# First unit's decay rows read straight from the sums and masked by GpSimd; two weight steps moved

## The reference, cut to what matters

```
proj = hidden_states @ in_proj_w.T                  # gate, xBC, dt
xBC  = silu(depthwise_conv(xBC, 4 taps))            # x, B, C
dt   = clip(softplus(dt + dt_bias), 0.001, 100)
cs   = cumsum(dt * A, inside a chunk of 128 tokens)
Lmat = where(tril, exp(cs[l] - cs[s]), 0)
Y    = ((C B^T) * Lmat) @ (x * dt) + contribution of the chunk before + x * D
out  = groupwise_rms_norm(Y * silu(gate)) @ out_proj_w.T
```

## Time and profile before

| | us |
|---|---|
| median of 3 runs | 2258.12 |
| the profiled execution | 2259.13 |
| its span | 2257.3 |
| PE busy | 2115.1 (94%) |
| DVE busy | 1571.0 (70%) |
| ACT busy | 1187.8 (53%) |
| POOL busy | 806.2 (36%) |

### The profile page before, as it was taken

One profiled execution on the slowest core, in us unless ns is written; L12 is line 12 of the kernel. 1 busy time (PEld: TensorE's weight loads), 2 busy tenths in 40 slices (PEclk: granted clock), 3 DMA queues, 4 the chain that ended last, 5 costly groups with the idle time before them and its releaser, 6 DMA issues. The chain is left out here.

```text
span 2257.3 us, 38134 instructions
## 1 busy us (share of the span) xinstructions
PE 2115.1 (94%) x11176; PEld 1596.0 (71%) x11176; DVE 1571.0 (70%) x3186; ACT 1187.8 (53%) x2846; POOL 806.2 (36%) x680
## 2 busy tenths in 40 slices
PE   6899998998888999999999999999999999987998
PEld 4555555545667777877777787777787787766877
DVE  3666665565688599589589778858958958845345
ACT  4554545413575377377467547647737746642330
POOL 4352523211154145235325425424524533431230
PEclk8799998999999999999999999999999999989999
DMA  6000000002989587697867958758769776602101
GB/s 248 11 1 10 7 1 1 1 0 73 244 212 219 110 230 189 114 230 183 158 184 190 183 141 205 176 114 226 190 108 234 184 147 187 152 22 103 46 10 38
DMA packets 242994, 286.94 MB, mean 127 GB/s; under 512 B 9440, under 2 KB 211424, under 8 KB 242144
## 3 DMA queue, kind: packets, MB, share of 16 engines
q1 hardware_dynamic: 242784, 284.43, 52.3%
HBM read 281.78 MB, written 104.60 MB: 171 GB/s over the span
## 5 line engine op out<-in xcount | busy, mean ns | idle before, releaser
L1719 PE MATMUL b_ps<-xh_keep,wh 128*128 128x512 f32 x1152 | 459.1, 399 | 3.5 <-DVE bc L1497 1.6
L1721 PE MATMUL b_ps<-xh_keep,wl 128*128 128x512 f32 x1152 | 449.7, 390 | 0.0
L1720 PE MATMUL b_ps<-xl_keep,wh 128*128 128x512 f32 x1152 | 449.0, 390 | 0.0
L1408 POOL TENSOR_TENSOR wl<-wraw,wh 128x512 fp32r<-128x512 f32 x144 | 186.8, 1297 | 384.3 <-ACT wh L1202 382.6
L1497 DVE SCALAR_TENSOR_TENSOR xs<-b_ps,par,xs 128x510 f32<-128x510 f32 (+2 forms) x384 | 284.5, 741 | 54.0 <-ACT xs L1223 40.6
L1525 DVE TENSOR_TENSOR decayed<-b_ps,b_scores 128x384 f32<-128x384 f32 x512 | 266.6, 548 | 45.3 <-ACT b_ps L1252 31.1
L1251 ACT ACTIVATE b_ps<-rows,ncs 128x256 f32<-128x256 f32 x512 | 238.9, 467 | 97.5 <-DMA rows<-skewed_rows 65.0
L1719 PEld LDWEIGHTS b_ps<-xh_keep,wh 128*128 128x128 f32 x1152 | 217.1, 188 | 50.0 <-issue 3.6
L1721 PEld LDWEIGHTS b_ps<-xh_keep,wl 128*128 128x128 f32 x1152 | 216.5, 188 | 46.9
L1720 PEld LDWEIGHTS b_ps<-xl_keep,wh 128*128 128x128 f32 x1152 | 217.2, 189 | 42.7
L1616 DVE SCALAR_TENSOR_TENSOR yl<-yg,par,yh 128x512 fp32r<-128x512 f32 x128 | 99.6, 778 | 202.2 <-ACT yh L1265 198.4
(11 more groups left out here) (228 smaller groups left out, 3967.4 us busy)
## 6 DMA issues: line engine op xcount, KB each, us to landing
rows<-skewed_rows SPq DMA_DIRECT2D x256, 384.0 KB, 4.2
skewed_rows<-sum_rows SPq DMA_DIRECT2D x63, 1024.0 KB, 12.1
wraw<-win_dram SPq DMA_DIRECT2D x144, 256.0 KB, 9.4
skewed_rows<-sum_rows SPq DMA_DIRECT2D x63, 512.0 KB, 14.1
qkv_or_out_weights<-wout_dram SPq DMA_DIRECT2D x8, 2048.0 KB, 16.4
w<-w_dram SPq DMA_DIRECT2D x2, 3584.0 KB, 23.3
fraw<-wgu_dram SPq DMA_DIRECT2D x11, 512.0 KB, 3.5
draw<-wd_dram SPq DMA_DIRECT2D x1, 2816.0 KB, 11.7
```

Source lines behind the costliest of these rows:

```text
L1408: nc.gpsimd.tensor_tensor(wl[:, n % RING, :], wraw[:, n % RING, :], wh[:, n % RING, :].bitcast(F32), ALU.subtract).then_inc(w_lo.sem, 1)
L1719: nc.tensor.matmul(out, w_h, x_h, start=(k == 0), stop=False)
L1720: nc.tensor.matmul(out, w_h, x_l, start=False, stop=False)
L1721: last = nc.tensor.matmul(out, w_l, x_h, start=False, stop=(k == KT - 1))
```

## The change

It has three parts, and they touch the start of the block, and the start of every group.

The decay rows of the first unit are no longer staged. `load_first` reads them from `sum_rows` straight into `rows`, every partition the same row (8 DMAs, 256 or 128 KB each, one with 1 KB runs and one with 512-byte runs for each sequence). What lies where l < s is then no longer -1e30, so GpSimd adds it: it makes a tile `below` (0 or -1e30) once, and for each sequence adds it to two blocks of 2 x 128 columns. It does so behind the low part of slice 4, with the low part of slice 5 behind the first sequence.

Slice 6 is loaded ahead of the sums. The wait for the padding moves behind the first rows.

In unit 0 of every group, ACT does the first tap ahead of `weights_hi(g, 6)`.

```
-            for n in range(3, 6):
+            for n in range(3, 7):
                 load_in(0, n)
             sp.wait_ge(sums_ready, 2)
             sp.dma_start(ssm["rows"][:, :, 0:SEQ], csT...).then_inc(kept, 16)
+            sp.wait_ge(kept, 16)
+            for b in range(BATCH):
+                load_first(b)
+            load_in(0, 7)
             sp.wait_ge(padded, 32)
-            sp.wait_ge(kept, 16)
-            for b in (BATCH - 1, *range(BATCH - 1)):
-                stage_first(b)
-            load_in(0, 6)
-            load_in(0, 7)
-            for b in range(BATCH):
-                load_rows(0, b)
             stage(1)
...
+            def load_first(b):
+                src = ssm["rows"].tensor
+                for at, shift, cols in ((0, 0, SEQ), (SEQ, P, P)):
+                    sp.dma_start(rows[:, b, :, at:at + cols],
+                                 bass.AP(tensor=src, offset=b * ROW + shift, ap=[[0, P], [BATCH * ROW, 2], [1, cols]]))\
+                        .then_inc(first_rows[b], 16)
...
-                    if more:
+                    if more and j:
                         weights_hi(g, 6 + 2 * j)
                     if h:
                         tap(ph, gn, h[0], ...)
                     if not j:
+                        weights_hi(g, 6)
                         next(e[0])
                         next(e[0])
...
-            for n in range(6):
+            nc.gpsimd.tensor_scalar(below[:], cst("tri"), 1.0, BIG, ALU.subtract, ALU.mult).then_inc(below_done, 1)
+            for n in range(5):
                 weights_lo(0, n)
+            pool.wait_ge(below_done, 1)
+            for b in range(BATCH):
+                pool.wait_ge(first_rows[b], 32)
+                for at in (0, SEQ):
+                    block = rows[:, b, :, at:at + P]
+                    last_ = nc.gpsimd.tensor_tensor(block, block, below[:]..., ALU.add)
+                last_.then_inc(rows_loaded[b], 16)
+                if b == 0:
+                    weights_lo(0, 5)
```

More of the change, by code:

```diff
@@ L1011, in ssm_layer @@
         ssq = sb("ssq", [P, TOK])
+        below = sb("below", [P, P])
         rs = sb("rs", [P, 3, NT])
@@ L1084, in ssm_layer @@
         staged = [sem(f"staged{k}") for k in range(8)]
-        first_staged = [sem(f"first_staged{b}") for b in range(BATCH)]
+        first_rows = [sem(f"first_rows{b}") for b in range(BATCH)]
+        below_done = sem("below_done")
         sums_ready = sem("d_sums")
@@ L1133, in load_rows @@
                     return
-                if n:
-                    g, j = (n - 1) // UNITS, (n - 1) % UNITS
-                    ph = Phase("loop", g, g) if g < LOOPS else Phase("epi", 0, g)
-                    sp.wait_ge(*bk.filled(ph, f"E{j}_{b}_1"))
-                    sp.wait_ge(staged[n % 8], 32 * ((n - 1) // 8 + 1))
-                else:
-                    for k in (b - 1, b):
-                        sp.wait_ge(first_staged[k % BATCH], 32)
+                g, j = (n - 1) // UNITS, (n - 1) % UNITS
+                ph = Phase("loop", g, g) if g < LOOPS else Phase("epi", 0, g)
+                sp.wait_ge(*bk.filled(ph, f"E{j}_{b}_1"))
+                sp.wait_ge(staged[n % 8], 32 * ((n - 1) // 8 + 1))
                 sp.dma_start(rows[:, b], bass.AP(tensor=ssm["skewed"].tensor, offset=n % STAGED * P * WIDE + b * ROW,
@@ L1446, in steps @@
                         out_weights_lo(g, 0)
-            for n in range(6):
+            nc.gpsimd.tensor_scalar(below[:], cst("tri"), 1.0, BIG, ALU.subtract, ALU.mult).then_inc(below_done, 1)
+            for n in range(5):
                 weights_lo(0, n)
+            pool.wait_ge(below_done, 1)
[3 more added lines that the diff above has]
+                    block = rows[:, b, :, at:at + P]
+                    last_ = nc.gpsimd.tensor_tensor(block, block, below[:].unsqueeze(1).to_broadcast([P, 2, P]), ALU.add)
+                last_.then_inc(rows_loaded[b], 16)
+                if b == 0:
+                    weights_lo(0, 5)
             with nc.Fori(0, LOOPS, engines=bass.OrderedEngineSet([pool.engine]), hint_back_edge=True) as i:
```

5 lines of the change are left out of this document (removed).

## The result

| | before | after |
|---|---|---|
| median, measured together | 2257.06 us (5 runs, 2251.16 to 2258.63) | 2240.04 us (5 runs, 2237.76 to 2247.59) |
| the profiled execution | 2259.13 | 2237.76 |
| its span | 2257.3 | 2235.9 |

The ratio is 0.9935, with a 95% interval of 0.9916 to 0.9954. The two medians lie 17.0 us apart; the ratio takes 14.7 of the 2257.06 us (10.4 to 19.0), and 12.0 were forecast.

A forecast was written before the change was run, and what follows sets the result against it. PE bounds the kernel on average, but a chain of DMA round trips bounds group 0; ending it 11.9 us sooner at no cost takes the median from 2258.1 to 2246.1 us, range 2242.5 to 2252.5.

The forecast's parts named there:

- Part 1, the first rows: Start of group 0: with the copies out of the queue, staging 1 lands at 578.3 instead of 590.23, 11.9 us sooner.
- rival of slow first rows: Start of group 0: first rows as slow as the old copies, 131 GB/s; gain 6.9 us, time 2251.2, chance 0.14.
- Part 2, the next round: Group 0, second round: staging 2 is issued by 580.8 instead of 592.67, so it follows 11.9 us sooner.
- the sign of ACT's gate: Sign of a wrong forecast: staging 2 more than 3 us behind unit 1's rows, held by ACT's use of old rows.
- Both limits: Issue of staging 2: ACT done with unit 0's rows allows 580.8, the landing of staging 1 allows 580.7.
- The rival in which the queue gains more: Group 0's queue: staging 2 starts with its issue, up to 4 us more gain, some 2243.5 us; chance 0.12.
- "still some 8 us": Sign of a right forecast: ACT's wait for rows in unit 2 stays, since rounds keep their 17.4 us pace.
- Part 3, PE isn't the limit: Group 0: PE could end at 672.4, the DMA chain at 682.4; PE's own 7.8 or 8.8 us is not the gain.
- Part 4, the masks: POOL in unit 0: 8 additions of 0.65 us, 5.2 in all, hidden; by the interference rule 11.7 instead of 11.9 us.
- Part 5, the exchange in later groups: Unit 0 of seven later groups: tap ahead of split costs 0, with 1.2 us of cover; 4.3 us if cover were gone.
- The slower rival: ACT's exchange costs 0.6 us in each of 7 later groups and group 0 gains nothing; 2262.4 us, chance 0.05.
- The sum: Whole kernel: group 0's shift of 11.9 us is passed on whole, nothing paid; the median becomes 2246.1 us.

The follow-up runs named there:

- e6: Changed kernel with the 8 DRAM to DRAM copies put back in SP's queue between the first rows and staging 1; 2255.13 us, 1.0008.
- e9: Changed kernel with four extra, waited-for GpSimd additions ahead of each sequence's two masks; 2247.37 us, 0.9967.
- e8: Changed kernel with only the direct first rows: slice 6 loaded behind them again, ACT in its old order; 2240.91 us, 0.9939.
- e3: Changed kernel without ACT's exchange: high part of slice 6 ahead of the tap again in every group; 2248.18 us, 0.9940.
- e10: Changed kernel with group 0's 2 MB of output weights loaded in unit 4 instead of unit 1; 2241.79 us, 0.9949.
- e12: Changed kernel with the second unit's rows also read directly and group 0's output weights loaded in unit 4; 2244.28 us, 0.9953.
- e13: Changed kernel with the second unit's rows also direct, their masks behind the low parts of slices 6 and 7; 2237.59 us, 0.9925.
- e15: Changed kernel, unchanged, third trace and third set of times; 2240.45 us, 0.9940.
- e2: Changed kernel, unchanged, second trace and second set of times; 2248.68 us, 0.9947.
- e4: Kernel before with ACT's exchange alone, tap ahead of the high part of slice 6; 2261.17 us, 0.9998.
- e5: Kernel before with ACT's exchange and slice 6 loaded ahead of the sums, first rows still staged; 2256.07 us, 1.0001.
- e7: Changed kernel with stagings 1 and 2 issued at the start and one more staging in flight in group 0; 2241.85 us, 0.9948.

## Where the prediction was right, and the step that failed

**Part 1, the first rows.** Right. Rows of unit 1 went out at 576.60, where 578.3 was the forecast, with sums that landed 1.5 us sooner; from the sums 18.5 us against 18.7, over three traces 19.1. The sum of bytes left one slice out (slice 8, issued at 566.61 behind staging 1): from 558.08 to 576.60 some 3.7 MB moved (199 GB/s for 18.52 us) where 3.4 were counted, and so the landing in time owes a little to luck. The first rows' own rate shows only in 559.00 to 562.00: 140 GB/s at a DMA share of 0.51, as the copies of before began (126 GB/s at 0.57 in 560.60 to 562.60). With slice 7 and staging 1 behind them the windows are at 206 and 212 GB/s, near the 223 taken. The rival of slow first rows falls by the rows of unit 1, which it had after 583.

**Part 2, the next round.** Right, and as tight as it was said to be. Staging 2 stood 2.4 us behind those rows (579.04), 2.5 in the second trace. In the third it stood 3.7 us behind, over the 3 us that were named as the sign of ACT's gate, and the later rounds took it back. Both limits that were said to lie side by side do: e6 moves the first and e9 the second, and either costs. The rival in which the queue gains more is not seen in its place: the rows of unit 2 go out 11.7 us sooner in the mean, as those of unit 1 (11.5). ACT's wait for them, "still some 8 us", was 5.88, 7.90 and 4.61 us (before 8.34, 9.50 and 7.61). ACT's wait for slice 6 is gone, but e8 shows that it would not have mattered: with a wait of 5.30 us left there, the gain is the same.

**Part 3, PE isn't the limit.** Right by e6. Turn 0 moved by 8.0 us in the mean where 7.8 or 8.8 was said (9.0, 9.0 and 6.1, trace by trace), and the end of the group by more, with the chain.

**Part 4, the masks.** Wrong in size, and without effect on the sum. A pair took 1.40 to 1.43 us when alone, 0.70 each; 0.65 was the estimate. POOL of the changed kernel:

```profile
563.00 1.90 POOL L1452 TENSOR_TENSOR rows<-rows,below 128x256 f32<-128x256 f32 x2 [5.42 <-DMA rows<-sum_rows]
564.85 1.73 POOL L1404 TENSOR_TENSOR wl<-wraw,wh 128x512 fp32r<-128x512 f32 x1
```

DVE beside it:

```profile
563.61 0.68 DVE L1513 SCALAR_TENSOR_TENSOR xs<-tx,xs 128x512 f32<-128x512 f32 x1
564.46 0.98 DVE L1513 SCALAR_TENSOR_TENSOR xs<-tx,xs 128x512 f32<-128x512 f32 x1 [0.16 <-ACT tx L1234]
```

The pair that met DVE took 1.90 instead of 1.40, the split 1.73 instead of 1.29, and one silu 0.98 instead of 0.68. That is the meeting that the rule of the Trainium skill (SBUF — State Buffer, "Who interferes with whom") foretold, at 0.3 us for DVE. The DVE silu at 563.61 ran at its 0.68 inside the pair's span: there it was POOL that lost the 0.5 us.

In six of the twelve traces of kernels with direct rows the meeting went worse (e3, e6, e10, e12, e13, and e15, the third trace of the changed kernel): the two silus of x took 2.85 to 2.96 us together, 1.37 in before. POOL of e15, then DVE, then PE, and a window (columns as in the earlier trace rows):

```profile
563.72 1.74 POOL L1404 TENSOR_TENSOR wl<-wraw,wh 128x512 fp32r<-128x512 f32 x1
```

```profile
564.23 1.78 DVE L1513 SCALAR_TENSOR_TENSOR xs<-tx,xs 128x512 f32<-128x512 f32 x1
```

```profile
567.73 0.70 PE L1763 MATMUL b_ps<-bc 128*128 128x256 f32 x2 [2.33 <-DVE b_scores L1556]
```

```profile
568.60:571.60 3.00, 3.00 (x10) 2.43 (x9) 2.26 (x4) 0.00 (x0) 2.20 (x4) 0.53 1.15 235
```

The silu ends 0.5 us behind the split, so it took 1.1 us more than its 0.68. PE waits 2.31 to 2.44 us in these six traces instead of 1.0, and behind that wait its granted clock is at half, 0.52 to 0.54 over 3 us; with the wait of 1.31 us in e2 it stays at 1.00. The first turn comes 15.9 to 16.0 us after the sums instead of 13.1 to 13.4. So the masks cost PE up to 2.7 us in unit 0, where the prediction's rule came to 0.2. The chain covers it: e15 has its group 1 after 204.1 us and its gain like the others. In these traces staging 2 also stands further behind the rows of unit 1: 3.7 us in e15, 3.4 in e3 and 4.0 in e10, but 2.5 in e6, whose rows come late.

**Part 5, the exchange in later groups.** Right by the times: cost 0, within the interval of e4. The lines of group 1, beside the earlier trace rows:

```profile
758.39 0.78 ACT L1218 ACTIVATE xs<-b_ps,par 128x512 f32<-128x512 f32 x1 [8.99 <-PE b_ps L1727]
759.07 0.62 ACT L1197 ACTIVATE wh<-wraw 128x512 fp32r<-128x512 f32 x1
...
763.09 0.48 ACT L1246 ACTIVATE b_ps<-rows,ncs 128x256 f32<-128x256 f32 x1 [2.04 <-DVE decayed L1531]
```

ACT is ahead of DVE still, and DVE does not wait for it: its decays begin at 762.34, the first exponentials stand at 759.59. The slower rival, which rested on this, falls with e4 and e3.

**The sum.** This is the step that failed: "11.9 us sooner, nothing paid", taken as the whole gain, on the ground that what group 0 ends with is passed on whole because PE is the bound behind it. The term measured 11.5 us where it was worked out, and 14.6 at the start of group 1. The mechanism held; the size of the shift that it hands on did not. Of the 3.1 us between, 1.7 lie behind the last turn: from the last turn to the first turn of group 1 before took 84.9, 82.9 and 84.3 us, after 81.8, 82.4 and 82.8 (the other staged kernels, e4 and e5, 84.0 and 83.8; the other nine with direct rows 80.9 to 82.7). PE is idle there for 3.6, 2.7 and 2.8 us before, and for 1.5, 2.1 and 1.3 after (length less busy time). One window of each, before and then after:

```profile
694.29:779.19 84.90, 81.30 (x384) 66.49 (x385) 52.07 (x84) 35.50 (x65) 26.32 (x20) 0.98 0.73 150
```

```profile
680.18:761.98 81.80, 80.27 (x384) 65.56 (x385) 51.90 (x84) 35.07 (x65) 26.39 (x20) 1.00 0.76 155
```

So the prediction stopped at the last turn, 694.27, and passed its shift on unchanged; the scans behind it waited for rows too (2.88 us in before's line above, 1.47 and 1.97 in its other two traces, against 0.30, 0.94 and none over 0.8 after). The waits are shown by the lines and the three traces of each (e4 and e5 have 2.46 and 2.26). That they go because the chain is earlier is not shown: e6, whose last turn is as late as in before, has no such wait and 82.6 us either. The other 1.4 us, between the rows of unit 1 and the last turn, are not settled: the last turn alone scatters by 3 us among traces of one kernel. The last 2.7 us, behind group 1's first turn, are within the scatter as a whole: before alone has 1476.1 to 1479.9 there, and the other kernels with the direct rows 1472.9 to 1479.5. They lie in groups 1 to 6, where the two kernels' traces do not overlap, and where PE is not the only bound, as it still stops for rows once in each group (e3 above). Whether the change has a part in them is open.

The second thing that was short is the range. It was built from the costs of the steps and had no term for the measurement itself. By the ratio of the first comparison and the 2258.12 us shown, the time is 2243.4 us (2239.2 to 2247.7), inside the range; the median that was taken, 2240.04, is outside, and later medians of the same kernel were 2248.68 and 2240.45, on two chips. That the median fell out of the range is in part chance: 13.4 us by the mean ratio are 1.4 more than the forecast.

## What to carry to other kernels

Where a stage is a chain of DMA round trips in one queue, count what stands in the queue ahead of the first link: its bytes moved every later stage here, even bytes that nobody waits for, and taking away an engine's stall there gave nothing. Follow the shift to the point where the next bound takes over, past the last event of the pattern, since the tail of the stage can have waits of the same kind. And give the range a term for the scatter between executions, beside those for the costs.

## What the runs showed of the hardware

- Transfers in which all 128 partitions read one row of DRAM, in runs of 1 KB and 512 bytes, began at 140 GB/s with half of the DMA share (0.51), much as DRAM to DRAM copies of such runs did (126 at 0.57). With other transfers behind them the windows showed 206 to 212.
- One queue carried a round of some 3.7 MB in 17 us when each round waited for the one before, and in 13.5 to 14.7 us with one more staging in flight (e7).
- A 256-column fp32 addition on POOL took 0.70 us, the split of 512 columns 1.29. A meeting cost POOL up to 0.5 us in one operation and DVE 0.3, or 1.1 in a silu that came behind the split's start (e15).
- In six traces PE stood for 2.3 to 2.4 us and its granted clock was then at half for some 3 us (0.52 to 0.54); after 1.3 us in e2 it stayed at 1.00.
- The medians of one kernel differed by 8 us between two chips, more than half of the whole gain; the three ratios, each on one chip, by 0.0012.
